# Output projection of an attention block: one f32 product made into three products of f16 halves, with the side work of a group moved around it

## What is computed

```python
x = L0_attn_x                                   # (4, 1024, 128) f32
x = x + layernorm(attn(layernorm(x), wq, wk, wv, wo))
x = x + layernorm(ffn(layernorm(x), ...))       # linear, SwiGLU, mixture of 8 experts, linear, SwiGLU

def attn(x, wq, wk, wv, wo):                    # 16 heads of 64, rotary embedding, causal
    q, k, v = x @ wq.T, x @ wk.T, x @ wv.T
    probs = softmax(where(causal, rope(q) @ rope(k).T * 64 ** -0.5, -inf))
    out = (probs @ v)                           # (4, 1024, 16 * 64)
    return out @ wo.T                           # the output projection, (4, 1024, 128)
```

## Time and profile before

| | |
|---|---|
| median of 3 runs | 1192.29 us |
| profiled execution, its own time | 1189.41 us |
| its span | 1187.5 us |
| attention, first to last score of the 16 groups | 62.38 to 936.84 us |
| last products of the attention, then the ffn | to 947 us, then to 1187.5 us |
| busy share of the span: PE, DVE, ACT, POOL | 93%, 81%, 81%, 80% |

### The profile page before, as it was taken

One profiled execution on the slowest core, in us unless ns is written; L12 is line 12 of the kernel. 1 busy time (PEld: TensorE's weight loads), 2 busy tenths in 40 slices (PEclk: granted clock), 3 DMA queues, 4 the chain that ended last, 5 costly groups with the idle time before them and its releaser, 6 DMA issues. The chain is left out here.

```text
span 1187.5 us, 36496 instructions
## 1 busy us (share of the span) xinstructions
PE 1110.2 (93%) x14311; PEld 800.0 (67%) x14311; DVE 959.2 (81%) x2195; ACT 956.4 (81%) x2205; POOL 951.1 (80%) x1064
## 2 busy tenths in 40 slices
PE   4689999999999999999999999999998788999996
PEld 1256777777777777777777777777776555666663
DVE  7789787978879797979788797979895359767977
ACT  7767989889797979798897979798887767756574
POOL 3569899999999999999999999999784567434663
PEclk9689999999999999999999999999998999999999
DMA  6761525252533425152515345252611000000011
GB/s 194 167 151 38 144 49 132 73 126 57 143 82 99 106 75 145 39 142 73 134 48 143 79 103 121 61 145 54 163 32 39 15 23 2 1 1 1 2 37 36
DMA packets 50475, 97.24 MB, mean 82 GB/s; under 512 B 8512, under 2 KB 25152, under 8 KB 46272
## 3 DMA queue, kind: packets, MB, share of 16 engines
q1 hardware_dynamic: 50304, 94.92, 31.6%
HBM read 58.47 MB, written 34.60 MB: 78 GB/s over the span
## 5 line engine op out<-in xcount | busy, mean ns | idle before, releaser
L916 POOL TENSOR_TENSOR Plo<-P,Phi 128x512 f16<-128x512 f32 (+3 forms) x634 | 531.6, 866 | 68.1 <-ACT P L566 66.4
L563 ACT ACTIVATE Phi<-psS 128x512 f16<-128x512 f32 (+3 forms) x768 | 394.6, 514 | 125.3 <-PE psS L413 74.1
L566 ACT ACTIVATE P<-psS 128x512 f32<-128x512 f32 (+3 forms) x634 | 313.8, 496 | 0.0
L435 PE MATMUL psO<-V,Plo 128*128 128x65 f16 x2304 | 289.2, 194 | 0.0
L431 PE MATMUL psO<-V,Phi 128*128 128x65 f16 x2304 | 288.6, 193 | 0.6 <-POOL Plo L916 0.6
L433 PE MATMUL psO<-V,Phi 128*128 128x64 f16 x2304 | 287.5, 192 | 0.0
L402 PE MATMUL psS<-Q,K 128*128 128x512 f16 (+3 forms) x768 | 252.8, 329 | 17.6 <-DVE Plo L742 13.0
L431 PEld LDWEIGHTS psO<-V,Phi 128*128 128x128 f16 x2304 | 216.1, 98 | 42.5 <-POOL Plo L916 1.4
L791 DVE TENSOR_REDUCE pmax<-psX 128x1 f32<-128x512 f32 x384 | 242.1, 681 | 0.2
L433 PEld LDWEIGHTS psO<-V,Phi 128*128 128x128 f16 x2304 | 214.9, 97 | 31.2 <-issue 1.1
L435 PEld LDWEIGHTS psO<-V,Plo 128*128 128x128 f16 x2304 | 214.4, 97 | 0.0
(11 more groups left out here) (215 smaller groups left out, 2500.7 us busy)
## 6 DMA issues: line engine op xcount, KB each, us to landing
k_way<-HL SPq DMA_DIRECT2D x64, 256.0 KB, 3.9
K<-k_way SPq DMA_DIRECT2D x32, 512.0 KB, 8.4
q_way<-HL SPq DMA_DIRECT2D x60, 256.0 KB, 3.7
Q<-q_way SPq DMA_DIRECT2D x15, 1024.0 KB, 11.8
K<-k_way SPq DMA_DIRECT2D x32, 256.0 KB, 4.3
Q<-q_way SPq DMA_DIRECT2D x30, 256.0 KB, 5.3
out<-y SPq DMA_DIRECT2D x8, 256.0 KB, 2.2
y<-in_x SPq DMA_DIRECT2D x3, 512.0 KB, 10.4
```

The lines of the kernel that those rows point to most:

```text
L435: mm = nc.tensor.matmul(O, M.Plo[:, U % NP_, k * P:(k + 1) * P], V[:, HD:2 * HD + 1], start=False, stop=j == t, skip_group_check=True)
L563: nc.scalar.activation(M.Phi[:, U % NP_, 0:w], X, ACT.Exp, scale=SCALE)
L566: nc.scalar.activation(full, X, ACT.Exp, scale=SCALE).then_inc(S.exp_done, 1)
L916: nc.gpsimd.tensor_tensor(M.Plo[:, U % NP_, 0:w], M.P32[:, U % NP_, 0:w], M.Phi[:, U % NP_, 0:w], ALU.subtract).then_inc(S.lo_pool, 1)
```

## The change

`OT` and `wo` become pairs of f16 tensors, high half and low half. A `wo` item is now 24 f16 products instead of 8 f32 ones: high by high, low by high, high by low. After a `tr` item ACT writes the high half, and DVE makes the low half from the bank and frees it: 4 further DVE instructions per group, 64 in all. The f32 weights are loaded into the second half of `OT`'s space, and split once in group 0 by ACT (step 20, 128x1024) and POOL (step 26, 128x1024). The tables are laid out anew: one `qk` from step 1 to 0, one `v` from 24 to 31, the second turn of the second pair of heads from 16 to 12, the other two turns from 33 and 46 to 34 and 45, sixteen of the 36 `mx` by one or two steps; DVE does its part of `v` one step later, and POOL its low halves of the rotated rows one step earlier.

```diff
-REST_LAG = 5
+REST_LAG = 4
-QK_STEPS = (1, 2, 7, 11, 16, 17, 23, 27)
-V_STEPS = (5, 24, 35, 46)
-LN_STEPS = (16, 32)
-MX_STEPS = (8, 8, 9, 10, 11, 12, 13, 14, 15, 15, 17, 18, 19, 19, 20, 20, 21, 21,
-            22, 23, 25, 25, 26, 28, 29, 29, 30, 31, 33, 34, 36, 36, 37, 38, 38, 40)
+QK_STEPS = (0, 2, 7, 11, 16, 17, 23, 27)
+V_STEPS = (5, 31, 35, 46)
+LN_STEPS = (16, 33)
+MX_STEPS = (7, 8, 8, 8, 9, 10, 12, 13, 14, 15, 16, 17, 18, 19, 20, 20, 21, 21,
+            22, 23, 25, 26, 27, 28, 29, 29, 30, 31, 33, 34, 36, 36, 38, 39, 39, 40)
-DVE_LAG = {}
+DVE_LAG = {'v': 1}
-TR1_STEPS, WO_STEPS, TR0_STEPS = (10, 16), (17, 18), (33, 46)
+WO_HALVES = ((0, 20), (0, 26))
+TR1_STEPS, WO_STEPS, TR0_STEPS = (10, 12), (17, 18), (34, 45)
...
                     for k in range(4):
                         for c in range(CH):
                             t = 4 * half + k
-                            mm = nc.tensor.matmul(X[:, k * P:(k + 1) * P], M.OT[:, c, t * P:(t + 1) * P],
-                                                  M.wo[:, CH * og + c, :], start=c == 0, stop=c == CH - 1)
+                            for q, (wi, xi) in enumerate([(0, 0), (0, 1), (1, 0)]):
+                                mm = nc.tensor.matmul(X[:, k * P:(k + 1) * P], M.OT[:, xi, c, t * P:(t + 1) * P],
+                                                      M.wo[:, wi, CH * og + c, :], start=c == 0 and q == 0,
+                                                      stop=c == CH - 1 and q == 2)
...
-                    nc.scalar.copy(M.OT[:, a[0], a[1] * BANK:(a[1] + 1) * BANK], X).then_inc(free(item), 1)
+                    nc.scalar.copy(M.OT[:, 0, a[0], a[1] * BANK:(a[1] + 1) * BANK], X).then_inc(S.turn_hi, 1)
...
+                if (s, u) == WO_HALVES[0]:
+                    act.wait_ge(S.wo_in, 16)
+                    nc.scalar.copy(M.wo[:, 0], wo32).then_inc(S.wo_hi, 1)
...
+                elif kind == "tr":
+                    dve.wait_ge(S.turn_hi, turn[item] + 1)
+                    if turn[item] == 0:
+                        dve.wait_ge(S.wo_lo, 1)
+                    cols = slice(a[1] * BANK, (a[1] + 1) * BANK)
+                    nc.vector.tensor_tensor(M.OT[:, 1, a[0], cols], X, M.OT[:, 0, a[0], cols],
+                                            ALU.subtract).then_inc(free(item), 1)
...
+                if (s, u) == WO_HALVES[1]:
+                    pool.wait_ge(S.wo_hi, 1)
+                    nc.gpsimd.tensor_tensor(M.wo[:, 1], wo32, M.wo[:, 0], ALU.subtract).then_inc(S.wo_lo, 1)
...
-            sp.dma_start(M.wo[:], I["wo"]).then_inc(S.wo_in, 16)
+            sp.dma_start(wo32, I["wo"]).then_inc(S.wo_in, 16)
...
-        M.wo = sb(stack, "wo", [P, HEADS * HD // P, D], F32)
+        M.wo = sb(stack, "wo", [P, 2, HEADS * HD // P, D], F16)
-        M.OT = sb(stack, "OT", [P, CH, T], F32)
+        M.OT = sb(stack, "OT", [P, 2, CH, T], F16)
```

More of the change, by code:

```diff
@@ L313, in attention_block @@
     weights = (M.wkq[:, 0], M.wkq[:, 1], M.wv)
+    ot32 = M.OT[:].rearrange("p w a n -> p (w a n)").bitcast(F32)
+    wo32 = ot32[:, TT * D:2 * TT * D].rearrange("p (k d) -> p k d", d=D)
+    turn = {}
+    for key in steps:
+        for item in at.get(key, []):
+            if item[1] == "tr":
+                turn[item] = len(turn)
     w32 = M.P32[:].rearrange("p a n -> p (a n)").rearrange("p (k n) -> p k n", k=3)
@@ L526, in side @@
                     if s == 1 and half == 0:
-                        pe.wait_ge(S.wo_in, 16)
+                        pe.wait_ge(S.wo_lo, 1)
                     taken(pe, (s - 1, "tr", 0, half))
@@ L627, in junk @@
             def junk(n):
-                to = M.On if n < 3 * TT else M.OT
                 k = (n - TT) % (2 * TT)
-                return to[:].rearrange("p a n -> p (a n)")[:, k * D:(k + 1) * D]
+                if n < 3 * TT:
+                    return M.On[:].rearrange("p a n -> p (a n)")[:, k * D:(k + 1) * D]
+                return ot32[:, k * D:(k + 1) * D]
             def x_sums(b):
@@ L1961, in build @@
         S.wo_in = sem("wo_in")
+        S.wo_hi = sem("wo_hi")
+        S.wo_lo = sem("wo_lo")
+        S.turn_hi = sem("turn_hi")
         S.w_lo_pool = sem("w_lo_pool")
```

## The result

The changed kernel takes 1175.03 us (median of 4 runs, 1174.23 to 1175.73) beside 1191.47 us before: a ratio of 0.9868, 95% interval 0.9851 to 0.9885, so 16.4 us or 1.3% faster. The forecast was 9.1 us faster, 1183.2 us. Its profiled execution took 1174.23 us, 15.2 us less than that of before.

What follows compares the result with a forecast made beforehand. PE was taken as the bound, 52.1 us of work and 1.8 of waiting a group. Regular groups -6.0, five others -2.5, ends -1.6, once only +1: -9.1 us from 1192.3 gives 1183.2 us, range 1175 to 1197.

Steps and rivals of the forecast that it cites:

- pair rate of 81 ns: Rival: the new `wo` products take 81 ns each, so PE saves nothing; +4 us, 1196; chance 0.02.
- Regular groups: Eight groups (3, 6, 7, 8, 10 to 13): -1.05 us of products, +0.3 of waiting, -0.75 each, -6.0 together.
- Steps 7 to 12: More reductions and low halves on DVE; PE's scores of step 11 wait longer; net +0.2 us a group.
- Steps 19 to 29: One reduction fewer behind the `wo` items and no `v`; PE's waits for reductions go: -0.3 us a group.
- Steps 34 to 38: First `mx` of step 36 waits for the bank DVE's low half frees: 0.7 us for 0.3, +0.4 a group.
- Steps 40 to 47: PE waits for ACT's exponentials and a rest behind them, as before: 0.
- Groups 1, 2, 4, 5 and 9: Groups 54.8 to 56.1 us long that wait more for others: -0.5 us each, -2.5 together.
- Group 0: Splitting `wo` once, on ACT and POOL: +0 to +1, taken as +1 us; no `wo` item there.
- The ends: Last group some -0.7 us, group 14 -0.5, the chain at the very end -0.4: -1.6 us.
- PE gets all of it: Rival: lag and new places remove as much waiting as low halves bring; -14.3 us, 1178; chance 0.20.
- POOL as the bound: Rival: POOL's work and waits keep a group at 53.9 us; -0.5 to -1.5 us, some 1191; chance 0.13.
- The banks of `psX`: Rival: low halves waiting for ACT hold up reductions and PE; +0.75 us a group, +9 us, 1201; chance 0.17.

Runs made afterwards that it cites:

- f1: Old tables and lags with the 24 products, but without DVE's low halves (low 16 bits left out of the result): 1176.63 us, ratio 0.9884.
- e2: The kernel before with only the new tables and lags, f32 products and no low halves: 1189.05 us, ratio 0.9989.
- e1: The changed kernel with all tables and lags of the kernel before, so products and low halves alone: 1200.31 us, ratio 1.0081.
- e5: The changed kernel without the low halves on DVE, ACT's copy freeing the bank (low 16 bits left out): 1173.60 us, ratio 0.9857.
- f2: The changed kernel with old tables and lags, except the new places of the transposes (10, 12 and 34, 45): 1189.84 us, ratio 0.9996.
- e10: The kernel before with the first `qk` item moved from step 1 to 0 in group 0 alone: 1189.14 us, ratio 0.9984.
- e9: The changed kernel with step 8's third maxima item moved on, row (7, 8, 8, 9, 10, 11, 12): 1180.65 us, ratio 0.9914.
- g2: The changed kernel with step 8's third maxima item moved one step only, row (7, 8, 8, 9, 9, 10, 12): 1178.26 us, ratio 0.9897.
- e6: The changed kernel with `REST_LAG` back at 5: 1175.17 us, ratio 0.9869.
- e4b: The changed kernel with each low half made twice on DVE, first into a tile nothing reads: 1210.06 us, ratio 1.0165.
- e7: The changed kernel without the lag of `v` on DVE: 1180.08 us, ratio 0.9910.
- f3: The changed kernel with the transposes back at steps (10, 16) and (33, 46): 1193.22 us, ratio 1.0027.

## Why the prediction was right, and where its sizes were off

**The time: inside the range, by luck in part.** The forecast was 1183.2 us with a range from 1175 to 1197, and 1175.03 lies on its edge; by the terms that the prediction names for that edge (1178, less 2 us) it would have been 1176. The gain, 16.4 us, is outside the -4 to -12 us that had a chance of 0.48. Of the 6.1 us that the sum missed in the profiled execution 4.3 are group 0, which has little to do with the products.

**Direction and products: right.** The products came out as costed, 56 ns each and 1.05 us a group: the item takes 1.34 us, and f1 has the whole of it, 53.91 to 52.88. The pair rate of 81 ns is ruled out by the same row.

**Regular groups: -6.8 us for a forecast of -6.0.** I took 0.3 us of new waiting a group; it is 0.05 in group 7 and 0.2 in the mean of the eight. By the stretches of the prediction, in group 7:

- *Steps 7 to 12*, +0.2 forecast. 0.54 us of waiting became 0.75, at step 8 and not at step 11, and 0.11 stand at step 13. The new tables did it, since e2 without low halves has much the same, 0.86, at step 8. Right in size, but not by the wait that I had named: PE's scores of step 11 waited 0.41 us for the rest of step 8, I added 0.3, and in the changed kernel that wait is gone. PE was held at step 8 already, for a `qk` item's product on DVE (0.40) and a reduction (0.28).
- *Steps 19 to 29*, -0.3 forecast: some 0.1 us less. Too large.
- *Steps 34 to 38*, +0.4 forecast: 0.17 less (0.30 to 0.13). This is the stretch where the reasoning failed. The bank of step 34's turn is free when the prediction says, 3.6 us after the step's start (the low half from 493.00 to 493.6, the step from 490.03). But I gave that bank to the first maxima item of step 36. The items go round three banks, and behind the transposes come `v`, the first and then the second of these items, so it is the second that takes it; it reaches PE 0.3 us later and waits 0.10 us, where I had 0.7 for the two. In the old order, with the transposes at 33, it is the first that takes it, and the stretch has 0.84 us in e1. But there too the first comes just after the bank is free (507.63, the low half from 506.72 to 507.3), and it is the second that waits, for the reduction that ScalarE's late copy has put back behind the low half. A late low half costs PE through what stands behind it on DVE, and the place of the transposes decides it.
- *Steps 40 to 47*, 0: 0.49 and 0.50.

DVE was forecast at 47.6 us a group and has 47.19. That it has room was right, the reason was not: the prediction let the lag take away DVE's 2.4 us of waiting at `v`, and e2 and e5, which have the lag, still wait 2.3. The low halves themselves take up that time.

**Groups 1, 2, 4, 5 and 9**, -2.5: -3.6. They gain 0.7 us each, near the regular ones; that they wait more for others did not hold them back as much as I allowed.

**Group 0: the largest miss, +1 forecast and -3.3 measured.** Two terms. The split of `wo` costs 0.1 us and not 1: group 0 takes 67.4 to 67.6 us with it in e1, f1 and f2, and without it before; 64.26 with it and 64.12 without in the changed order. And I costed the `qk` item's move from step 1 to 0 at nothing, since I read it from a regular group. In group 0 it stands ahead of a wait of 2.29 us and takes a step's scores out of that wait (e10: 2.3 us). The last 1.1 us are also the new tables' and not the products', since e2 has 64.12: with them the two waits of step 8 that e10 shows are gone.

**The ends**, -1.6: groups 14 and 15 together -1.8 us for -1.2. That all of it shows in group 14 comes from where the cut between the groups lies. In the kernel before, the first product of group 15 waits for a transfer of its row maxima, and the first one of its fourth unit for a rest on DVE:

```profile
888.25 0.39 PE L402 MATMUL psS<-Q,K 128*128 128x512 f16 x1 [1.42 <-DMA Q<-mrow]
893.26 0.29 PE L402 MATMUL psS<-Q,K 128*128 128x128 f16 x1 [2.75 <-DVE Plo L742]
```

In the changed kernel the first wait is gone and the second is longer by as much:

```profile
878.98 0.29 PE L410 MATMUL psS<-Q,K 128*128 128x128 f16 x1 [4.34 <-DVE Plo L756]
```

Without these 1.6 us group 14 is at -0.6 and group 15 at -1.2, for -0.5 and -0.7. What lies behind them is 0.3 us longer, for -0.4. There the chain is as forecast, with its numbers against the earlier trace rows: the products of the last two items take 2.84 us for 3.81, and the wait ahead of them, now for DVE's low half, 1.06 for 0.33, so 0.2 us are gained. The remainder is of the size by which that stretch differs from run to run (below).

**The rivals.** *PE gets all of it* is nearest to the result in its time (1178, measured 1175). But its reason, that layout and low halves cancel, holds only for the pair (to 0.05 us in group 7, 0.2 in the mean of the regular ones). *POOL as the bound* is out: 51.12 us busy of 52.91, and no load of PE in the group waits for it; f1, where POOL is at 97%, says the same. The reading by busy share that the Trainium skill gives ("Perfetto Trace Analysis", Identifying the Most-Contended Engine) would have named POOL: in the changed kernel's group 7 PE's weight loads are busy 39.66 of 52.91 us, or 75%, and POOL 97%. No run here bears it out. *The banks of `psX`* was the rival that would have come true without the new tables, with its own price: three low halves in PE's way, +0.75 us a group and +9 us forecast, +0.71 us and +9.8 us measured in e1. DVE's wait for ScalarE was 0.8 to 0.9 us at two of the low halves and nothing at the one of step 10. The threshold of 1.05 us of new waiting holds too: f2 has 1.0 and is at 0.9996. I gave this case 0.17 and wrote nothing down that speaks against it; what each number of the new tables does about it I did not work out.

## What to carry to other kernels

Faster products and the side work that they bring have to be tried together with the order around them: here the products alone lost 0.8%, the order alone won 0.1%, and both won 1.3%. What a step of side work costs is set by whether the engine reaches it when its input is there (in the old order DVE stood 0.8 to 0.9 us for ScalarE twice a group, with the reductions that free the next banks queued behind; four low halves cost 1.74 us a group there and 0.1 in the new order), not by its 0.6 us or by that engine's share of busy time. And an item's move is to be costed also in the first group, where a wait that no regular group has can stand right behind it.

## What the runs showed of the hardware that I had not expected

The granted clock behind the attention differs between kernels whose code there is the same: it was full in the two windows shown of the kernel before, and 0.83 and 0.66 in those of e2. From the last score product to the end the kernel before takes 250.7 us, the changed kernel 251.0, e1, f1, f2, e5 and e9 250.9 to 251.3, g2 252.1, e6 252.7, and e2, e10, e4b, e7 and f3 253.5 to 255.8. PE's work there isn't changed by any of them, beyond the last output items. In that time the low level lasts 17 us in f3 (255.8) and 10 us in e2 (253.5), but 6.8 us both in f1 (251.1) and in e10 (253.7), so how long it lasts does not by itself give the time. Group 15 has the same: in e10, with the full clock throughout, it takes 46.44 us, and in the kernel before, at a mean of 0.89, 48.59. In none of these is the cause shown. What is shown is that 3 to 5 us can come and go behind the attention and 2 us in its last group, as much as e2 or e10 had won in group 0, and that a part of such a change is better read from the regular groups than from the whole.
